# Attention of a two-layer network: loops over batches replaced by written-out batches

## The reference

```python
scores = einsum('bhqd,bhkd->bhqk', q, k) / sqrt(8)
scores = scores + rel_bias                       # the first attention only
scores = where(causal, scores, -inf)             # the first and the third
attn = softmax(scores, axis=-1)
x = x + einsum('bhqk,bhkd->bhqd', attn, v) @ WO + bO
```

## Time and profile before

| | |
|---|---|
| median of 3 executions | 5252.44 us (5251.10 to 5255.83) |
| the profiled execution | 5253.41 us |
| its span, first to last instruction | 5251.6 us |
| busy, share of the span: PE, PEld, DVE, ACT, POOL | 80%, 40%, 65%, 54%, 38% |
| mean granted TensorE clock | 0.910 of full speed |
| instructions in the trace | 108370 |
| DMA | 489.50 MB, mean 93 GB/s |

### The profile page before, as it was taken

The page is one execution under the profiler, slowest core; times in us unless marked ns, Lnnn a source line. Parts: engine busy times, 40 slices in busy tenths (PEclk is TensorE's granted clock), DMA queues, the critical chain, the costliest instruction groups (busy, mean ns, idle before and its releaser), DMA issues. The chain is left out here.

```text
span 5251.6 us, 108370 instructions
## 1 busy us (share of the span) xinstructions
PE 4205.7 (80%) x31331; PEld 2104.6 (40%) x31332; DVE 3399.0 (65%) x8427; ACT 2852.9 (54%) x5677; POOL 1970.2 (38%) x2539
## 2 busy tenths in 40 slices
PE   6499999899576766779868888886987788878698
PEld 3144444452222222226312222225973333333597
DVE  3488888448799899894478777762116766665212
ACT  7255555666555555557747676672324455555232
POOL 3000000011677777770403433344536144444452
PEclk9699999999899899899979899897999888888799
DMA  7522222005100000000532222224656332332466
GB/s 259 140 74 73 73 73 74 23 0 197 65 26 26 26 26 26 26 26 0 203 90 81 70 77 72 70 62 133 212 173 224 92 84 79 83 84 62 143 213 191
DMA packets 530984, 489.50 MB, mean 93 GB/s; under 512 B 160546, under 2 KB 468067, under 8 KB 530560
## 3 DMA queue, kind: packets, MB, share of 16 engines
q1 hardware_dynamic: 512496, 448.21, 28.7%
q0 software_dynamic: 18160, 37.42, 2.0%
HBM read 324.32 MB, written 161.09 MB: 92 GB/s over the span
## 5 line engine op out<-in xcount | busy, mean ns | idle before, releaser
L1539 ACT ACTIVATE p_probs<-p_t_ps 128x512 f32<-128x512 f32 (+1 forms) x2304 | 1142.9, 551 | 778.4 <-PE p_t_ps L1353 230.8
L2122 PE MATMUL p_y_ps<-p_prod,c_ident 128*128 128x512 f32 x1024 | 555.8, 669 | 304.1 <-DVE p_prod L2307 299.2
L1366 PE MATMUL p_o_ps<-p_probs,p_v_st 128*32 128x256 f32 (+3 forms) x8704 | 775.8, 432 | 7.4 <-ACT p_o_sb L1525 7.0
L1335 PE MATMUL p_t_ps<-p_t_q,p_t_k 50*128 50x512 bf16 (+3 forms) x3072 | 540.9, 351 | 263.1 <-ACT p_probs L1539 154.8
L1603 DVE TENSOR_REDUCE p_row_max<-p_s_ps 128x1 f32<-128x512 f32 x1024 | 644.8, 681 | 150.4 <-PE p_s_ps L1304 116.0
L2256 POOL TENSOR_TENSOR p_dbx<-p_dtx,p_b_sb 128x512 f32<-128x512 f32 x512 | 632.8, 1272 | 120.6 <-ACT p_b_sb L2153 120.6
L2298 DVE TENSOR_TENSOR_SCAN p_state<-p_da,p_dbx 128x512 f32<-128x512 f32 x512 | 599.2, 1207 | 94.5 <-ACT p_da L2191 76.9
L1241 POOL TENSOR_TENSOR p_v_st<-p_v_raw,p_ones 128x128 f32<-128x128 f32 x192 | 87.5, 456 | 1414.1 <-PE p_o_ps L1366 1358.7
L1304 PE MATMUL p_s_ps<-p_s_k,p_s_q 48*128 48x512 bf16 (+3 forms) x3072 | 508.8, 356 | 122.6 <-DVE p_row_max L1600 49.1
L1600 DVE CUSTOM_DVE_ANT_0 p_tried<-p_s_ps,c_mask_row 128x512 bf16<-128x512 f32 (+3 forms) x1024 | 450.0, 486 | 218.1 <-PE p_s_ps L1304 159.6
L1600 DVE CUSTOM_DVE_ANT_0 p_tried<-p_s_ps,p_s_bias 128x512 bf16<-128x512 f32 (+3 forms) x1024 | 449.6, 485 | 133.8 <-PE p_s_ps L1304 131.3
(11 more groups left out here) (295 smaller groups left out, 7084.9 us busy)
## 6 DMA issues: line engine op xcount, KB each, us to landing
p_wb<-in_w SPq DMA_DIRECT2D x142, 512.0 KB
p_s_q<-stack_q SPq DMA_DIRECT2D x384, 96.0 KB
p_s_k<-stack_k SPq DMA_DIRECT2D x384, 96.0 KB
p_t_q<-stack_q SPq DMA_DIRECT2D x384, 96.0 KB
p_t_k<-stack_k SPq DMA_DIRECT2D x384, 96.0 KB
mamba_inputs<-p_out SPq DMA_DIRECT2D x17, 1536.0 KB, 5.7
p_inp<-mamba_inputs SPq DMA_DIRECT2D x17, 1536.0 KB
p_raw<-routed_rows SPq DMA_DIRECT2D x142, 130.0 KB
```

The lines of the kernel that those rows point to most:

```text
L1335: mm = pe.matmul(out[r], t_k[rows, g % 2, pair, c * P:(c + 1) * P], t_q[rows, g % 2, pair, first:first + width], start=True, stop=not mask ...
L1366: mm = pe.matmul(o_ps[32 * j:32 * j + 32, at:to], v_st[:, g % 2, c, j, :], probs[:, g % 2, j, place[c] + at - first:place[c] + to - first] ...
L1539: act.activation(exps, tile, ACT.Exp, scale=scale).then_inc(expd, 1)
L2122: pe.matmul(y_ps[:, h], w["ident"], prod[:, k_slot(n, h, RS)], start=(n == 0), stop=(n == STATE - 1)).then_inc(acc_mm, 1)
```

## The change

In `attend`, four loops on registers become Python loops, so that every batch is written into the program: those of SP, TensorE, ScalarE and VectorE. The order of the work on each engine is the same, and so is each wait's meaning. Batch numbers, waits and addresses become constants in the instructions. POOL's stream is the same in every instruction.

```diff
--- before.py
+++ after.py
@@ -1209,7 +1209,7 @@
                     step(b, g)
             if rt:
                 rt.fill_spares(sp)
-            with sp.Fori(2, TO) as b:
+            for b in range(2, TO):
                 for g in range(4):
                     step(b, g)
             for g in range(4):
@@ -1440,7 +1440,7 @@
             for b in range(FROM):
                 for g in range(4):
                     step(b, b, g)
-            with pe.Fori(0, (TO - FROM) // UNROLL) as turn:
+            for turn in range((TO - FROM) // UNROLL):
                 for u in range(UNROLL):
                     for g in range(4):
                         step(UNROLL * turn + (FROM + u), FROM + u, g)
@@ -1558,7 +1558,7 @@
             for b in range(FROM):
                 for g in range(4):
                     step(b, b, g)
-            with act.Fori(0, (TO - FROM) // UNROLL) as turn:
+            for turn in range((TO - FROM) // UNROLL):
                 for u in range(UNROLL):
                     for g in range(4):
                         step(UNROLL * turn + (FROM + u), FROM + u, g)
@@ -1687,7 +1687,7 @@
             for b in range(FROM):
                 for g in range(4):
                     step(b, b, g)
-            with dve.Fori(0, (TO - FROM) // UNROLL) as turn:
+            for turn in range((TO - FROM) // UNROLL):
                 for u in range(UNROLL):
                     for g in range(4):
                         step(UNROLL * turn + (FROM + u), FROM + u, g)
```

## The result

| | before | after |
|---|---|---|
| median, lowest to highest, us | 5251.77, 5236.01 to 5255.83 (4 runs) | 5187.67, 5182.43 to 5196.16 (4 runs) |
| ratio of the two, 95% interval | | 0.9885, 0.986 to 0.991 |
| the profiled execution, its span, us | 5253.41, 5251.6 | 5182.43, 5180.6 |
| mean granted clock | 0.910 | 0.919 |

The account below looks back on a forecast made before the run. It took stage 1 as nearly full on TensorE and VectorE, and stage 2 as stalled by TensorE's jumps to unloaded code. Terms -12.6 + 1.2 = -11.4 us gave 5241.0 us on the median, range 5229 to 5253.

Parts of the forecast that it names:

- Stage 1, +1.2 us: Stage 1, biased attention: newly loaded code costs 0.09 us in each of 13 turns, +1.2 us.
- The term for code: Stages 1 and 3, where code no longer stays: half of 0.18 us a turn in stage 1, 0 in stage 3.
- Stage 2, -12.6 us: Stage 2, unmasked attention: without loop ends twelve batches take 55.5 us each, 666.0 against 678.6, so -12.6 us.
- whatever the smaller engines wait for behind theirs lies beside TensorE's stall: Loop ends, stage 2: smaller engines' waits behind their own branches coincide with TensorE's stall; VectorE's branch takes 56 ns.
- the lower bound of 7.1 us: Stage 2: only the matmuls' idle time at three jumps goes and the clock drops stay, -7.1 us.
- The upper bound, -19.2: Stage 2: every batch like the first pair's 54.95 us, 659.4 against 678.6, so -19.2 us.
- Register arithmetic, 0: Attention loops: turn-dependent waits and addresses become constants, worth 0, since register instructions run during waits or with matmuls queued.
- Stage 3, 0: Stage 3, rotary attention: loading of code put at 0, as matmuls run only 38 to 41 of some 50 us.
- The jumps of stages 1 and 3: TensorE's 25 jumps there take 0.21 us, no stall; the skill's rule would add 86 us gain, given no chance of its own.
- Given back: Rival, chance 0.18: idle time goes, clock drops stay, new code costs 0.18 us every turn; -2.6 us, 5249.8 us.
- TensorE waits at each new packet: Slower rival, stages 1 and 3, chance 0.06: 0.25 us at each of 110 packets, +27.5; total +14.9, 5267.3 us.
- The stage 3 rival: Stage 3's mix of turns shifts: three more short, 5231.4 us, chance 0.12; three more long, 5250.6 us, chance 0.10.

Follow-up runs that it names:

- SyncE runs: sp_alone and sp_again: kernel before with only SyncE's queue written out in all three stages, chip C; 5064.0 and 5063.0 us, ratio 0.9998 each.
- after_mamba: The change with VectorE's loop of mamba_scan written out too, against the kernel before on chip E: 5173.1 us against 5252.6, ratio 0.9846.
- all_but_pe: VectorE, ScalarE and SyncE written out, TensorE in its loops, against the kernel before on chip E: 5203.1 us against 5252.6, ratio 0.9902.
- all_but_dve: TensorE, ScalarE and SyncE written out, VectorE in its loops, against the kernel before on chip D: 5212.6 us against 5242.8, ratio 0.9948.
- pe_alone: Kernel before with TensorE alone written out in all three stages, chip A: 5076.3 us against 5061.4, ratio 1.0034.
- dve_alone: Kernel before with VectorE alone written out, chip C: 5029.5 us against 5064.7, ratio 0.9933.

## Why the prediction was wrong

The forecast, 5241.0 us, missed the measured time by 53 us. The two profiles are 71.0 us apart, 60 more than forecast, and three places make that up: stage 2 gave 14.4 us more than forecast, and stage 3 gave 25.7 and mamba_scan 20.3, both of which stood at nothing in the sum.

**Stage 1, +1.2 us: the sum was right by luck, the terms were not.** A turn rose from 47.43 to 47.53 us, 13 x 0.1 = 1.3. It is made of +0.44 for TensorE and -0.36 for VectorE in a turn. The term for code, half of the 0.18 us of the first turn, was too small against 0.44; why that first turn, with as many packets, lost only 0.18 is open. The loop's register arithmetic, put at 0 by a comparison of first groups, was worth 0.36 us a turn on VectorE together with its jump, behind which 0.09 us idle stand and no packet of code comes.

**Stage 2, -12.6 us: a second stall stood behind the first.** The step "whatever the smaller engines wait for behind theirs lies beside TensorE's stall" failed. I read VectorE's branch at 56 ns and did not look at the instruction after the next, where its 3.5 us stand. On chip C TensorE alone, with its stalls gone, takes 613.4 us against 611.1 and 617.9 in the SyncE runs, so not even the lower bound of 7.1 us shows, and VectorE alone 598.6. On chips with late signals both count: on D the change has 645.5 us, and 662.5 without VectorE; on E after_mamba has 658.2, and all_but_pe, without TensorE's part, 674.2. That is 17 and 16 us, where the two profiles before have 678.6 and 669.7 in all. The upper bound, -19.2, was made from batches that had the late signals in them, so it was no floor.

**Register arithmetic, 0.** It is 0 where I looked, the third group of a batch. GpSimd's transfers go out in groups 0 and 3, and there the looped kernel sees signals later on such chips. The comparison was of the right kind at the wrong place; group 0 of batch 15 against that of batch 14, in the same trace, would have shown 2.3 us, and against the mean of batches 3 to 14 (12.6 us) 1.6.

**Stage 3, 0.** The forecast took its long turns (50.9 us, clock 0.83) and short ones (47.8) as given and let only their mix move. All twelve are long: the same work takes 487.5 / 12 = 40.6 us where no signal is late. The change took 25.7 us off; its waits behind late signals are shorter, and the clock rose from 0.86 to 0.89. VectorE's part, the change against all_but_dve on chip D, is 11.2 us. TensorE's is not seen: on chip E all_but_pe has 570.2 us and after_mamba 570.3. By subtraction, then, the larger rest is of ScalarE or SyncE; no run on such a chip has either of them alone, so this is argued and not shown, and which of the two it is stays open.

**What was left out: mamba_scan, in code that the diff does not touch.** Nothing in the prediction asked what the added instructions move. VectorE's loop of mamba_scan had its target near the end of a piece of code by chance. Of the 20.3 us between the two profiles about 10 are this wait.

**The jumps of stages 1 and 3** were read rightly: TensorE's go back in 0.21 us and writing them out brought nothing (491.9 us in stage 3 against 487.5, a cost). The Trainium skill, Runtime: NRT & Kernel Launch, section "Instruction fetch mechanics", gives TensorE a store of 2048 instructions and most other engines one of 512, and calls full unrolling preferable. For TensorE the trace agrees: its stage-2 body with 1170 weight loads and as many matmuls stalls, and its stage-1 body with 602 of each does not. VectorE's bodies in mamba_scan, 508 records a turn, and in stage 2, 397, should fit by that, and the trace disagrees: they wait at every jump. The preference doesn't hold for TensorE in this kernel, as pe_alone is 1.0034 of before. The section's blocks of 16 KiB are those of q8, while q14's are 8 KB.

**The rivals.** "Given back" and "TensorE waits at each new packet" both fell on these chips. The second is right in kind, though: 0.44 us for five packets is 0.09 us a packet, where 0.21 was needed to make the change slower; on chips A and C it does make TensorE alone slower. The stage 3 rival named the right stage and too small a size.

**The better version** is not shown on chips with late signals. after_mamba is at 0.9846 of before, between the change's own 0.9837 and 0.9891 on other chips: the 16 to 20 us that it saves in mamba_scan are there, but its stages 2 and 3 took 658.2 and 570.3 us, 7 to 16 and 2 to 9 more than the change's. Why is open; its VectorE code is moved again. On the chips without late signals the best kernel that ran is dve_alone (0.9933). The change as a whole was not run on one of those: an estimate from its single stages there (-10, -1 and +5 us) is a gain of 5 to 6 us, one from its single engines (VectorE -35, TensorE +9 to +15, ScalarE -5, SyncE -1 us) a gain of 26 to 32. The two don't agree, so what it does there is open.

## What to carry to other kernels

A stall at a loop's end has to be looked for on every engine, and at the instructions behind the branch, not in its duration: removing TensorE's, which ended first, brought nothing on chips A and C, and removing VectorE's did. Any change in the number of instructions moves all later loops of that engine, and here an untouched phase changed by 1% with it; pad such a phase with idle instructions before believing a cause. A gain measured on one chip may be another on the next: have the kernel before beside every run. Before a stretch is called normal, hold it against the same work elsewhere in the trace, here batch 15 against 14 and batch 2 against 3.

## What the runs showed of the hardware

- One program, one chip design, two speeds: 5061 to 5065 us on chips A and C (C twice) and 5232 to 5253 us on B, D and E. The difference lies in stages 2 and 3: per batch of stage 3, 40.6 us on A against 47.7 to 51.5 in the first profile, while mamba_scan and stage 1 are alike.
- On B, D and E signals from one engine to another came 0.3 to 1.5 us late while GpSimd issued indirect transfers of 0.95 us each; on A and C they were not late with the same transfers. The median was 1.1 to 1.2 us where all loops stood and 0.4 to 0.5 in the six traces with both ScalarE and SyncE written out.
- Where signals were late, TensorE's granted clock was lower too: 0.96 on A and C in stage 3, 0.86 before and 0.89 after on the others.
- VectorE's jumps to code that was not there show in its branch record with 50 to 74 ns only; in stage 2 the next record of its queue came 4.0 us later. In mamba_scan the engine went on 1.6 to 1.8 us behind the end of the 8 KB packet, and waited again, for 1.0 to 1.3 us, where the target lay so that a second packet was needed.
- TensorE's code written out cost 0.09 us for each 16 KB piece in stage 1 (0.44 us for five), net of what its loop had cost.
